# Attention scores of two heads as 64-row fp32r tiles beside each other, 512-column banks of row-maximum scores, and an order laid anew

## What is computed

```python
xn = _layernorm(x)
x = x + attention(xn) + ffn(xn)

# attention: 16 heads of 16, causal
q, k, v = xn @ Wq + bq, xn @ Wk + bk, xn @ Wv + bv      # per head
scores = einsum('bhtd,bhsd->bhts', q, k) * 16 ** -0.5
probs = softmax(scores + causal)
y = einsum('bhts,bhsd->bhtd', probs, v)                  # heads side by side
attention = y @ Wo + bo

# ffn: 8 experts, each token goes to its best two, hidden and inner size 256
top, selected = top_k(xn @ Wr, 2)
h = clip(silu(xn @ Wg[e]), -7, 7) * (xn @ Wu[e])
ffn = sum over the two e of softmax(top)[e] * (h @ Wd[e])
```

## Time and profile before

| | |
|---|---|
| time, median of 3 runs | 434.12 us (433.74 to 434.62) |
| time of the profiled execution | 434.04 us |
| its span, first to last instruction | 432.1 us, 8149 instructions |
| mean granted TensorE clock | 0.979 |
| busy: PE, DVE, ACT, POOL | 409.7, 329.6, 221.7, 195.7 us |
| moved by DMA | 71.3 MB, 165 GB/s |

### The profile page before, as it was taken

How to read it: one execution, slowest core, us unless ns; L and a number is a source line. 1 busy time by engine, 2 the same in 40 slices (tenths; PEclk the granted TensorE clock), 3 DMA queues, 4 the chain that set the end, 5 groups by cost and what they waited for, 6 DMA issues and landing times.

```text
span 432.1 us, 8149 instructions
## 1 busy us (share of the span) xinstructions
PE 409.7 (95%) x2755; PEld 247.9 (57%) x2755; DVE 329.6 (76%) x1043; ACT 221.7 (51%) x511; POOL 195.7 (45%) x223
## 2 busy tenths in 40 slices
PE   8999877998999999999999999999999999999993
PEld 8576423565345456565757567655766476656332
DVE  6726999999999775879387866788477989881686
ACT  0564262350665665646373465456465436537980
POOL 6321266575334168554793248415745265213420
PEclk9999899996999999999999999999999999999996
DMA  8179678868329059752595419915695344100682
GB/s 255 58 217 295 169 175 203 279 189 303 97 50 210 2 176 219 208 185 98 170 248 164 152 29 256 293 59 184 179 259 160 129 120 159 36 26 6 231 278 76
DMA packets 40372, 71.33 MB, mean 165 GB/s; under 512 B 5893, under 2 KB 30598, under 8 KB 40332
## 3 DMA queue, kind: packets, MB, share of 16 engines
q0 software_dynamic: 9360, 39.99, 29.7%
q1 hardware_dynamic: 27132, 26.76, 23.7%
q10 hardware_dynamic: 3840, 4.08, 3.2%
HBM read 55.85 MB, written 15.60 MB: 165 GB/s over the span
## 4 chain that ended last, share of the span: by engine, by line
PE 69%; DVE 20%; ACT 3%; DMA 3%; issue 3%; POOL 1%; POOLq 0%; SPq 0%; ACTq 0%; DVEq 0%
PE psum L1358 15%; PE psum L1319 14%; PE psum L1280 11%; PE psum L1299 10%; PE psum L1367 7%; DVE psum L1001 7%; DVE mxa L1004 5%; PE psum L1211 4%; PE psum L1235 3%; ACT probs L912 3%; PE psum L1341 2%; DMA bqk<-in_bqk 2%; PE psum L1348 1%; DMA x<-in_x 1%; DVE yt L1131 1%
## 5 line engine op out<-in xcount | busy, mean ns | idle before, releaser
L912 ACT ACTIVATE probs<-psum 128x512 f32<-128x512 f32 (+1 forms) x320 | 151.2, 581 | 52.3 <-PE psum L1299 51.8
L1001 DVE CUSTOM_DVE_ANT_0 psum<-psum,maskrow 128x128 f32<-128x128 f32 (+3 forms) x256 | 121.1, 504 | 7.7 <-PE psum L1280 7.5
L1280 PE MATMUL psum<-packk,packq 96*128 96x512 bf16 (+3 forms) x384 | 93.9, 331 | 4.0 <-DVE mxa L1004 1.9
L1004 DVE TENSOR_REDUCE mxa<-psum 128x1 f32<-128x512 f32 x128 | 87.6, 685 | 10.1 <-PE psum L1280 10.0
L1299 PE MATMUL psum<-packq,packk 99*128 99x512 bf16 (+3 forms) x384 | 89.1, 327 | 1.8 <-ACT probs L912 1.0
L1319 PE MATMUL psum<-probs,v 128*32 128x512 f32 (+3 forms) x768 | 74.0, 493 | 2.7 <-POOL probs L839 2.5
L1280 PEld LDWEIGHTS psum<-packk,packq 96*128 96x128 bf16 x384 | 34.7, 98 | 56.5 <-issue 19.1
L839 POOL TENSOR_SCALAR_AFFINE_SELECT probs<-probs 128x512 f32<-128x512 f32 (+1 forms) x48 | 40.8, 853 | 53.1 <-ACT probs L912 53.0
L1299 PEld LDWEIGHTS psum<-packq,packk 99*128 99x128 bf16 x384 | 32.9, 97 | 43.1 <-issue 13.5
L806 POOL DMA_INDIRECT xg<-xn_rows,token x39 | 37.7, 967 | 31.9 <-PE psum L1348 22.1
L1358 PE MATMUL psum<-xgt,wexp 128*128 128x128 f32 x384 | 47.3, 276 | 0.5 <-ACT xgt L919 0.2
(11 more groups left out here) (124 smaller groups left out, 476.6 us busy)
## 6 DMA issues: line engine op xcount, KB each, us to landing
qk_parts<-stage SPq DMA_DIRECT2D x24, 256.0 KB, 3.5
stage<-expert_rows SPq DMA_DIRECT2D x16, 256.0 KB, 4.7
packq<-qk_parts SPq DMA_DIRECT2D x16, 192.0 KB, 5.3
packk<-qk_parts SPq DMA_DIRECT2D x14, 192.0 KB, 7.7
x<-in_x SPq DMA_DIRECT2D x4, 512.0 KB, 5.6
packq<-qk_parts SPq DMA_DIRECT2D x16, 128.0 KB, 7.7
xn_rows<-probs ACTq DMA_DIRECT2D x4, 512.0 KB, 6.8
out<-x SPq DMA_DIRECT2D x16, 128.0 KB, 3.1
```

The source lines that it names most:

```text
L912: act.activation(probs[:, g % RING, h, 0:width], psum[:, bank, 0:width], ACT.Exp, scale=SCALE)\
L1001: ins = dve.tensor_tensor_reduce(out=chunk, in0=chunk, in1=maskrow[:, BANK - width:], scale=1.0, scalar=NEG, op0=ALU.add, op1=ALU.max, acc ...
L1004: ins = dve.tensor_reduce(into, chunk, op=ALU.max, axis=AX.X)
L1280: pe.matmul(psum[:, bank, 0:width], packq[0:MAXROW, u % SLOTS, i // HALF, h, P * (i % HALF):P * (i % HALF + 1)], packk[0:MAXROW, u % SLOTS ...
```

## The change

q and k are split into two fp32r parts instead of three bf16 parts: ACT writes the first, DVE the second; POOL and ACT's second copy have no more part in it. Three products of parts (48 rows) and two rows for the maximum make 50 rows. The four heads of a unit become two pairs; a pair's two heads lie at partitions 0 to 49 and 64 to 113, and each score of a pair is two matmuls on two 64-row tiles of the array, into two banks. Parts are stored per tile of q or k (one DMA) and loaded for each side by itself: 16 DMAs a unit instead of 12.

Row-maximum scores are packed to 512 columns in a bank: blocks of 128 and 384 columns, and of 256 and 256, share one, so a unit has 18 chunks of two banks each. Each block still has its own DVE instruction. The negated maximum has two parts and is transposed in fp32.

The planner gets one more PE mode, "r", for the new tiles, prices for changes between the modes, a window in which it prefers the due time over the earliest start (`patience`), new due times, four banks each for the two kinds of score, and other durations; so all lists change. The first q/k product waits for the weights alone and no longer for the bias.

```diff
-PARTS = 3
-RUNS = ((0, 0, 0, 3), (3 * HD, 1, 0, 2), (5 * HD, 2, 0, 1))
-PACKS = 2 * len(RUNS)
-MAXROW = 6 * HD
+PARTS = 2
+SIDES = 2
+PAIRS = UH // SIDES
+SIDE = P // SIDES
+RUNS = ((0, 0, 0, 2), (2 * HD, 1, 0, 1))
+PACKS = 2 * SIDES * len(RUNS)
+MAXROW = 3 * HD
 KROWS = MAXROW + PARTS
-CHUNKS = [(h, i, s) for c in range(2) for h in range(UH) for i in range(HALF * c, HALF * (c + 1))
-          for s in range(i * P // BANK + 1)]
+CHUNKS = [((p, i, 0),) for i in range(HALF, TB) for p in range(PAIRS)]
+for c in (0, 1):
+    closing = [*(((p, HALF * c, c), (p, HALF * c + 2, c)) for p in range(PAIRS)),
+               tuple((p, HALF * c + 1, c) for p in range(PAIRS)), *(((p, HALF * c + 3, c),) for p in range(PAIRS))]
+    CHUNKS = CHUNKS + closing if c else closing + CHUNKS
...
-ROOM = {"nat": 3, "s": 3, "y": 2, "qk": 2, "v": 2}
+ROOM = {"nat": 4, "s": 4, "y": 2, "qk": 2, "v": 2}
...
+                    if engine == "PE":
+                        at = max(at, now + SWITCH.get((mode, own), 5))
+                        due += PACE["stay"] * (own != mode)
+                    picks.append((at, due, key))
+                if picks:
+                    soon = min(picks)[0] + (PACE["patience"] if engine == "PE" else 0)
+                    pick = min((p for p in picks if p[0] <= soon), key=lambda p: (p[1], p[0], p[2]))
...
-SWITCH = {("b", "b"): 5, ("f", "f"): 15, ("b", "f"): 95, ("f", "b"): 20, ("b", "c"): 105, ("f", "c"): 105,
-          ("c", "b"): 110, ("c", "f"): 120}
-PACE = dict(attention=(60000, 405000), experts=(90000, 355000))
+SWITCH = {("f", "r"): 200, ("b", "r"): 200, ("c", "r"): 220, ("r", "f"): 180, ("r", "b"): 180, ("c", "f"): 185, ("c", "b"): 185,
+          ("r", "c"): 125, ("f", "c"): 106, ("b", "c"): 106}
+PAIR_NS = 18
+PACE = dict(a0=54.88, a1=370.21, m0=91.12, m1=308.83, spread=0.71, last=90.87, ahead=12.24, first=77.35,
+            first_step=0.85, later_qk=25.77, qk_step=7.41, v0=-14.58, v_step=2.91, routing=45.14, gather=-12.39,
+            fetch=-40.46, down=1.03, half=20.95, half_step=23.63, proj_step=3.12, load=105.68, pv=5.44, patience=0.2,
+            stay=5.78, keep=1)
...
-            pe(("nat", u, m), width / 2.4 + 2, after, due, ("nat", u, m), "b")
-            dve(("max", u, m), width * 1.04 + 72, [("PE", ("nat", u, m))], due, ("nat", u, m))
+            pe(("nat", u, m), width / 2.4 + PAIR_NS, after, due, [("nat", u, m, side) for side in range(SIDES)], "r")
+            for side in range(SIDES):
+                dve(("max", u, m, side), max_ns(m), [("PE", ("nat", u, m))], due, ("nat", u, m, side))
...
-        qk_d = nc.dram_tensor("qk_parts", [2, 2, PARTS, HD, H // 2, N], BF16).ap()
+        qk_d = nc.dram_tensor("qk_parts", [2, 2, PARTS, HD, H // 2, N], F32).ap()
-        packq = sb("packq", [P, SLOTS, 2, UH, BANK], BF16)
-        packk = sb("packk", [P, SLOTS, 2, UH, BANK], BF16)
+        packq = sb("packq", [P, SLOTS, 2, PAIRS, BANK])
+        packk = sb("packk", [P, SLOTS, 2, PAIRS, BANK])
...
-            def store(w):
+            def store(k):
+                b, grp, op, n = qk_tile(k)
+                wait_freed(sp, ("qk", k))
+                cols = slice(T * b + BANK * n, T * b + BANK * (n + 1))
+                sp.dma_start(qk_d[op, grp, :, :, :, cols].rearrange("r d h t -> (d h) r t"),
+                             stage[:, k // 2 % 2, op, :, :]).then_inc(qk_out[k // 2 % 2], 16)
...
-            def qk_lo_part(k):                                         # POOL
-                pool.wait_ge(qk_mid, k + 1)
-            def qk_mid_part(k):                                        # ACT
-                act.copy(stage[:, k // 2 % 2, stored(k, 1), cols], resid[:, k % 2, :]).then_inc(qk_mid, 1)
-            def qk_resid_part(k):                                      # DVE
+            def qk_lo_part(k):                                         # DVE
+                dve.scalar_tensor_tensor(part[:, stored(k, 1), :].bitcast(F32R), psum[:, bank, :], bqk[:, op, grp:grp + 1],
+                                         part[:, stored(k, 0), :], ALU.add, ALU.subtract).then_inc(freed[bank], 1)
...
             def natural(u, m):
+                blocks = chunk_blocks(m)
+                for p, i, s, width, at in blocks:
+                    for side in range(SIDES):
+                        rows = slice(SIDE * side, SIDE * side + MAXROW)
+                        fill = ("nat", u, m, side)
+                        bank, full = (FILL_AT[fill][0], filled[FILL_AT[fill][0]]) if at else wait_room(pe, fill)
+                        ins = pe.matmul(psum[:, bank, at:at + width],
+                                        packq[rows, u % SLOTS, i // HALF, p, P * (i % HALF):P * (i % HALF + 1)].bitcast(F32R),
+                                        packk[rows, u % SLOTS, s, p, 0:width].bitcast(F32R), start=True, stop=True)
+                        if at + width == blocks[-1][4] + blocks[-1][3]:
+                            ins.then_inc(full, 1)
...
-            def scores(g, h):
+            def scores(g, p):
+                for j, t0, width, at in blocks:
+                    for side in range(SIDES):
+                        rows = slice(SIDE * side, SIDE * side + KROWS)
+                        fill = ("s", g, PAIRS * side + p)
+                        ins = pe.matmul(psum[:, bank, at:at + width],
+                                        packk[rows, u % SLOTS, j // HALF, p, P * (j % HALF):P * (j % HALF + 1)].bitcast(F32R),
+                                        packq[rows, u % SLOTS, c, p, t0:t0 + width].bitcast(F32R), start=True, stop=True)
```

More of the change, by code:

```diff
@@ L26 @@
 BF16 = mybir.dt.bfloat16
+F32R = mybir.dt.float32r
 I32 = mybir.dt.int32
@@ L143, in neg_of, with neg_spans @@
     return min(c, 1) if u == 0 else u + 1
+def neg_spans(x):
+    _, c0, c1 = NEGS[x]
+    return [(0, PARTS)] if c1 - c0 == 2 else [(part, part + 1) for part in range(PARTS)]
 def negs_landed(x):
     u = NEGS[x][0]
-    return sum((1 if c1 - c0 == 2 else PARTS) for v, c0, c1 in NEGS[:x + 1] if v % SLOTS == u % SLOTS)
+    return sum(SIDES * len(neg_spans(y)) for y in range(x + 1) if NEGS[y][0] % SLOTS == u % SLOTS)
 HAND = 50
@@ L164, in __init__, with job @@
         self.last = {}
-    def job(self, engine, stage, ns, after=(), due=0, takes=None, frees=None, mode="", lag=None, size=0):
+    def job(self, engine, stage, ns, after=(), due=0, takes=(), frees=None, mode="", lag=None, size=0):
         lag = LAG[engine] if lag is None else lag
@@ L200, in run @@
                     if takes:
-                        room = [t for b, t in enumerate(banks) if b not in holder.values()]
-                        kind = takes[0]
-                        if not room or held.get(kind, 0) >= ROOM.get(kind, BANKS):
+                        room = sorted(t for b, t in enumerate(banks) if b not in holder.values())
+                        kind, want = takes[0][0], len(takes)
+                        if len(room) < want or held.get(kind, 0) + want > ROOM.get(kind, BANKS):
                             continue
-                        if kind != "y" and len(room) == 1 and not held.get("y"):
+                        if kind != "y" and len(room) < want + PACE["keep"] and not held.get("y"):
                             continue
-                        at = max(at, min(room))
+                        at = max(at, room[want - 1])
                     at = max(at, now)
[L209 to L213, removed]
+                    if engine == "PE":
[5 more added lines that the diff above has]
+                    pick = min((p for p in picks if p[0] <= soon), key=lambda p: (p[1], p[0], p[2]))
+                    if best is None or pick < best:
+                        best = pick
             assert best, ("stuck", [k for e in open_.values() for k in e][:20])
@@ L263, in pe @@
     def pe(stage, ns, after=(), due=0, takes=None, mode="f", lag=None):
-        job("PE", stage, ns, after, due, takes, None, mode, lag)
-    a0, a1 = PACE["attention"]
-    m0, m1 = PACE["experts"]
+        fills = [takes] if isinstance(takes, tuple) else takes or []
+        job("PE", stage, ns, after, due, fills, None, mode, lag)
+    a0, a1, m0, m1 = (PACE[name] for name in ("a0", "a1", "m0", "m1"))
     weight = [step_width(n) + 100 for n in range(NS)]
@@ L447, with fills_of @@
 FIRST_OF = {"qk1": "qk"}
-def fill_of(stage):
+def fills_of(stage):
     kind = stage[0]
@@ L715, in neg_rows @@
                 wait_freed(sp, ("neg", k))
-                for first, last in ([(0, PARTS)] if c1 - c0 == 2 else [(part, part + 1) for part in range(PARTS)]):
-                    dst = packq[MAXROW + first:MAXROW + last, u % SLOTS, c0:c1, :, :].rearrange("a c h t -> a (c h t)")
-                    rows = slice(UH * TB * first + UH * HALF * c0, UH * TB * (last - 1) + UH * HALF * c1)
-                    sp.dma_start(dst, negt[rows, :]).then_inc(neg_in[u % SLOTS], 16)
+                per = PAIRS * HALF
+                for side in range(SIDES):
+                    for first, last in neg_spans(k):
```

(3 more changed lines are left out.)

306 lines of the change are left out of this document (142 added, 164 removed).

## The result

The changed kernel takes **409.87 us** (median of 4, 408.86 to 411.59) where the kernel before takes 434.37 beside it: a ratio of 0.944 (0.9405 to 0.9475), 24.5 us less. The forecast was 393 with a range of 372 to 416: the sign and the range held, 17 of the 41 forecast us are missing. The profiled execution is the one of 411.59 us, span 409.8.

A forecast was written before the change was run, and what follows sets the result against it. It took PE as the bound from 140 to 400 us, with DVE fuller from 40 to 140. Start, pairing, shape changes and freed PE time summed to 434.0 - 3 - 44 + 15 - 9 = 393 us, range 372 to 416.

The forecast's parts named there:

- The bound: PE bounds from 140 to 400 us, busy 258.4 of 260; DVE is fuller from 40 to 140, 95.0 of 100.
- The pair: Score matmuls: two heads stream together at one head's cost, saving 44 us between 140 and 400 us (0 to 44).
- The start: Before the first row maximum: splitting ends sooner and stores leave earlier, saving 3 us (0 to 6).
- Freed PE time from 40 to 140 us: 18 us of PE time there could take expert tiles pulled in; half booked, 9 us saved (0 to 18).
- the worst end of the sum: Whole kernel, fp32r and pairing as taken, worst bounds of the terms: 434 - 0 - 44 + 20 - 0 = 410 us.
- the early terms: Savings before 140 us: 3 us from the earlier start and 9 us from freed PE time between 40 and 140.
- The changes of shape: Score-stretch borders on PE: 0.14 us at 130, 0.04 more at 82; 21.5 us, 15 of it from 140 to 400.
- DVE as the bound (372): Rival: the new order fills DVE at 95.0% as from 40 to 140 us, so DVE sets 372 us; chance 0.13.
- Single file (409): Rival: a pair's two weight loads go one behind the other, slowing narrow pairs by 16 us to 409; chance 0.16.
- The slower case (452): Rival: pairs gain nothing (fp32r at half rate or tiles in turn), changes of shape stay: 452 us; chance 0.10.
- PE busy: Sign that the forecast is right: PE's busy share of the span falls to about 88%, with DVE at 83%.

The follow-up runs named there:

- the new due times: Changed kernel with orders laid again under higher prices for changes of tile shape and due times searched anew: median 416.22 us, ratio 0.9629 to the kernel before.

## Why the prediction was right in sign and range, and 17 us short

- **The bound** was read rightly: PE is full from 140 us on, before and after. In the table the score columns and changes give -56.2 + 30.9 = -25.3 us of PE, and starts span 21.8 us less.
- **The pair**: halving 125.6 us in the whole kernel would give 62.8; measured 56.2. The step that took one fp32r pass at bf16's rate and the tiles together was right, a pair's pace is 0.231 instead of 0.218, and narrow pairs (128 columns at 0.060, not 0.22) show that the weights do not go in single file. Short by 6.6, of which 3.7 are the pace (384 pairs are 66.5 us).
- **The start** came as forecast where it was looked for: the first row maximum moved from 38.39 to 34.49, 3.9 us for 3.

```profile
34.49 0.30 DVE L1018 CUSTOM_DVE_ANT_0 psum<-psum,maskrow 128x128 f32<-128x128 f32 x1
34.70 0.14 DVE L1018 DVE_READ_ACCUMULATOR2_ANT mxa<- 128x1 f32 x1
```

- **Freed PE time from 40 to 140 us** was hardly used, and most of the start's lead is gone by 140 us as well: this is the step that failed most. The gate matmuls, the row-maximum scores and the softmax scores up to 140 us (length, busy us and count on PE and PEld, clock, DMA share, GB/s), before and then after:

```profile
0.00:140.00 140.00, 13.65 (x96) 12.99 (x96) 0.96 0.68 193
0.00:140.00 140.00, 30.71 (x122) 11.41 (x122) 0.96 0.68 193
0.00:140.00 140.00, 15.56 (x62) 5.26 (x62) 0.96 0.68 193
...
0.00:140.00 140.00, 14.02 (x96) 12.82 (x96) 0.95 0.69 214
0.00:140.00 140.00, 24.71 (x122) 12.13 (x122) 0.95 0.69 214
0.00:140.00 140.00, 14.63 (x72) 7.82 (x72) 0.95 0.69 214
```

  Of 624 gate matmuls 96 are done in both and of 384 row-maximum scores 122 in both; of 384 softmax scores it is 72 for 62. DVE's 91.6 of 100 us is no fuller than before. Booked were 9 us for the freed time and 3 for the start; of these 12 some 3 are there, as work that PE has done ahead (743 of its 2755 matmuls for 705). What held the kernel up before 140 us stays open: neither the removed wait for the store nor the lighter reductions on DVE won more than 3 us.
- **From 140 us on** lies the gain: the starts span 266.7 us for 288.6, 21.9 less, some 3 of which are that lead, where 44 - 15 = 29 were booked. The scores' own time falls by 46, for the booked 44. The changes of shape take 17 to 21 more, by the limits above, for the booked 15. Second heads that start late take 7, which had no term: the prediction named a pair's two banks, but looked for their cost only before 140 us. Other work and other waits make up the rest. So the time came out at the worst end of the sum, 434 - 0 - 44 + 20 - 0 = 410, with the early terms near nothing and the changes with the late heads above 20.
- **The changes of shape** in the whole kernel were set too low: 0.14 us for each of 130 borders and 0.04 more at 82, 21.5 us in all. There are 143 and 89, nearly as counted, and they add 30.9. The upper bound of 0.17, taken from a score's 386 ns less 218, priced an array that runs empty; it left out that the next shape's weights are not loaded meanwhile, so that the second matmul comes late too (0.10). Into scores it comes to 0.20, out of them to 0.30. The rows that would have told stood in the kernel before: its column tiles cost 0.11 at the border back to 128-row work and 0.10 at the start behind it, in 15 places; I read the one border (from scores into column tiles) that has next to nothing behind it. Short by 9.4.
- **Two ways to cut one shortfall**: over the whole kernel 6.6 and 9.4 come to 16 of the 17 us missing, by stretch some 9 before 140 us and some 10 behind it to the 19 that are missing between the two profiled executions (22 less instead of 41). They are not to be added, and it is chance that 62.8 - 21.5 is 41, as the forecast is with its 3 and 9. PE's net of 25 us shows nearly whole in the main change, an edit's in the experiments by a third to two thirds; why, is not shown.
- **The tail**: the last expert's down product starts at 364.4 for 397.1. A part of this goes back behind it, where 45 us are left instead of 35, as more attention is left then (80.2% of the softmax-score matmuls done for 85.2%). There ACT has long rows of exponentials:

```profile
369.59 9.22 ACT L931 ACTIVATE probs<-psum 128x512 f32<-128x512 f32 x20 [1.79 <-PE psum L1325]
...
390.42 10.03 ACT L931 ACTIVATE probs<-psum 128x512 f32<-128x512 f32 x22 [1.47 <-PE psum L1325]
```

  Whether a better balance of experts and attention would win this back was not shown: the new due times ended the experts earlier in the plan and were slower.

- **The rivals**: DVE as the bound (372) is out, since 33 us off DVE win 3. By the Trainium skill, "TensorEngine Tiling (Array Packing)", PSUM Bottleneck, the emptying of PSUM may become the limit once tiling has sped TensorE up; here it has not, as 33 us less of that reading on DVE moved the time by under 1%. Single file (409) gives the right time for a wrong reason. The slower case (452) does not apply; one row tile makes it so, at 453.21.
- **PE busy** was to fall to 88%; it stays at 95%. The share counts the time at changes as busy as well as work: PE's own time falls from 369 to 313 us in the table, and the share could not tell.

## What to carry to other kernels

Before small row tiles are mixed with full-array work, price each change by starts, at the border and at the start behind it, into and out of the shape: here 0.2 and 0.3 us, against 0.23 for a pair of 512 columns, so that changes took back about half of what pairing gave. Gather work of one shape into longer stretches and fill banks to 512 columns, which here was worth 10 us and more. Then check what a term of PE time is worth by adding or removing some: a third to two thirds showed, and a wait of 9 us that was removed showed nothing.

## What the runs showed of the hardware

- Two 64-row tiles with fp32r operands stream together: starts 3 ns apart in the median (within 10 ns in 308 of 382 pairs), 512 columns in 0.230 to 0.233 us, 128 in 0.060; four on one tile take 1.03 us where two pairs take 0.57.
- A change into or out of the 64-row tiles costs 94 to 199 ns at the border and 103 to 106 at the second start behind it (20 behind a change into column tiles); an eight-column matmul on 128 rows between two pairs adds 0.31 us, on 64 rows nothing that the time shows.
- At the change looked at, no weight load of the next shape runs beside the last matmul of the first: a gate matmul's load starts with it at 206.31, where in the kernel before it started with the last score at 201.00.
